# Condition numbers loaded once, W1's masks behind c's low halves, signs for two quarters, and 120 constant products ahead of the first conditioning

## What is computed

```
w = weights[conditions]                               # [128, 64, 64]
c = einsum('bct,bcd->bdt', x, w)                      # x: [128, 64, 512]
def ternarize(W):                                     # W1: [2048, 512], W2: [512, 2048]
    delta = 0.05 * max|W|; mask = |W| > delta
    alpha = sum(|W| where mask) / max(count(mask), 1)
    return alpha * sign(W) * mask
h = gelu(c @ ternarize(W1).T + b1)                    # exact gelu
y = h @ ternarize(W2).T + b2
scale = max|y| / 7 + 1e-8
out = x + clip(round(y / scale), -7, 7) * scale
```

## Time and profile before

| | |
|---|---|
| median of 3 runs | 1003.65 us (1003.36 to 1004.45) |
| the profiled execution | 1004.09 us |
| its span | 1002.2 us |
| PE busy | 925.8 us (92%) |
| DVE busy | 644.5 us (64%) |
| ACT busy | 547.3 us (55%) |
| POOL busy | 144.8 us (14%) |
| mean granted clock | 0.974 |

### The profile page before, as it was taken

How to read it: one execution, slowest core, us unless ns; L and a number is a source line. 1 busy time by engine, 2 the same in 40 slices (tenths; PEclk the granted TensorE clock), 3 DMA queues, 4 the chain that set the end, 5 groups by cost and what they waited for, 6 DMA issues and landing times.

```text
span 1002.2 us, 14662 instructions
## 1 busy us (share of the span) xinstructions
PE 925.8 (92%) x5136; PEld 440.1 (44%) x5136; DVE 644.5 (64%) x1024; ACT 547.3 (55%) x690; POOL 144.8 (14%) x187
## 2 busy tenths in 40 slices
PE   2999999999999999999999999999999999999700
PEld 2544444444444444444444444444444444444300
DVE  7998576665656666656657666665666665633493
ACT  6886728274473827365372827446382836536190
POOL 4400030301203030200203030110303030000000
PEclk9999999999999999999999999999999999999955
DMA  9501103012212102111210301121210301204899
GB/s 341 154 2 43 43 14 82 10 42 44 50 42 51 43 10 59 32 45 42 52 42 25 69 10 42 46 48 42 52 42 10 69 23 44 84 0 168 313 385 390
DMA packets 24318, 77.86 MB, mean 78 GB/s; under 512 B 3952, under 2 KB 4080, under 8 KB 23792
## 3 DMA queue, kind: packets, MB, share of 16 engines
q1 hardware_dynamic: 20032, 73.41, 24.6%
q0 software_dynamic: 3840, 3.94, 1.4%
q10 hardware_dynamic: 432, 0.34, 0.1%
HBM read 60.89 MB, written 16.78 MB: 77 GB/s over the span
## 4 chain that ended last, share of the span: by engine, by line
PE 80%; issue 9%; DVE 5%; ACT 2%; DMA 1%; POOL 0%; SPq 0%; DVEq 0%; POOLq 0%; ACTq 0%
PE ps L433 39%; PE ps L443 37%; PE ps L413 3%; PE ps L494 3%; ACT y L706 1%; DMA y<-in_L_ffn_W 1%; DVE st L907 1%; DVE wts L866 1%; DVE wts L1046 1%; DVE wts L756 1%; DVE y L1046 0%; SPq L275 0%; DVE yc L772 0%; POOL odd L354 0%; DVE wts L911 0%
## 5 line engine op out<-in xcount | busy, mean ns | idle before, releaser
L433 PE MATMUL ps<-yc,wts 128*128 128x512 f16 x2048 | 444.9, 379 | 0.0
L443 PE MATMUL ps<-wts 128*128 128x512 f16 x1792 | 391.4, 379 | 0.0
L433 PEld LDWEIGHTS ps<-yc,wts 128*128 128x128 f16 x2048 | 200.4, 98 | 241.5 <-ACT g L610 0.4
L756 DVE SCALAR_TENSOR_TENSOR wts<-g,st,wts 128x512 f16<-128x512 f32 x256 | 186.4, 749 | 140.2 <-ACT wts L615 138.5
L610 ACT ACTIVATE g<-ps,b1t,st 128x512 f32<-128x512 f32 x256 | 197.9, 774 | 123.3 <-PE ps L433 106.7
L443 PEld LDWEIGHTS ps<-wts 128*128 128x128 f16 x1792 | 173.4, 98 | 204.8
L615 ACT ACTIVATE wts<-g,st 128x512 f16<-128x512 f32 x256 | 181.0, 713 | 0.0
L597 ACT ACTIVATE xs<-yx,st 128x2048 f16<-128x2048 f32 x28 | 56.1, 2002 | 136.8 <-DVE st L790 136.8
L365 POOL PARTITION_ALL_REDUCE st<-st x46 | 21.8, 473 | 663.3 <-DVE st L725 416.1
L348 POOL DMA_INDIRECT odd<-in_L_cond_weights,odd x112 | 110.1, 983 | 41.5 <-issue 30.0
L761 DVE SCALAR_TENSOR_TENSOR y<-ps,st,b2b 128x512 f32 (+1 forms) x56 | 41.6, 747 | 79.8 <-PE ps L443 79.7
(11 more groups left out here) (131 smaller groups left out, 366.8 us busy)
## 6 DMA issues: line engine op xcount, KB each, us to landing
yx<-in_x SPq DMA_DIRECT2D x56, 512.0 KB, 6.3
wts<-in_x SPq DMA_DIRECT2D x10, 512.0 KB, 5.4
out<-wts SPq DMA_DIRECT2D x10, 512.0 KB, 14.0
y<-in_L_ffn_W SPq DMA_DIRECT2D x8, 512.0 KB, 8.8
wts<-in_x SPq DMA_DIRECT2D x4, 1024.0 KB, 5.0
y<-in_L_ffn_W SPq DMA_DIRECT2D x4, 1024.0 KB, 20.5
y<-in_x SPq DMA_DIRECT2D x3, 1024.0 KB, 9.4
out<-wts SPq DMA_DIRECT2D x3, 1024.0 KB, 13.0
```

The costliest lines, as they stand in the source:

```text
L433: last = nc.tensor.matmul(psH[:, j % HB, :], T1T[:, j // HC, k, j % HC * P:(j % HC + 1) * P], csp[:, a, k, :], start=(k == 0 and a == 0), ...
L443: last = nc.tensor.matmul(psY[:, r % 2, :], hsp[:, a, j, r * P:(r + 1) * P], T2T[:, j, :], start=(j == 0 and a == 0), stop=(j == HT - 1 an ...
L756: nc.vector.scalar_tensor_tensor(out=hsp[:, 1, j, :], in0=g[:, j % HB, :], scalar=s_h, in1=hsp[:, 0, j, :], op0=ALU.mult, op1=ALU.subtract ...
```

## The change

- The condition numbers are loaded as one row. DVE clamps the row, PE spreads it to 128 partitions with a product with a row of ones (into hidden tile 0's bank), and DVE makes the row numbers from there.
- x for block 0 is loaded ahead of the last two pieces of W1. b1 is issued behind ACT's first magnitude, b2 as before behind the last. ACT spreads block 0's weights and sums x ahead of the last two magnitudes, and the high halves of c ahead of all relus.
- POOL reduces the bound on c ahead of W1's maximum. DVE makes the scale of c ahead of the threshold. Masks 1 to 3 of W1 stand behind the low halves of c and the rest of quarter 0.
- The count of W1's masks is 64 products with one column each, behind hidden tile 2, and its partition sum is made in the all-reduce of the sums. The second conditioning stands behind hidden tile 3 instead of tile 0; its copies stand beside gelu 8 and 11.
- Quarters 2 and 3 of the ternary W1 are made as sign (ACT) times mask (DVE, f16). The first ternary quarter of W2 is made in two parts, with a signal for the first.
- PE runs 120 products of a constant tile, whose result isn't used, ahead of the first conditioning.

```diff
-        condb, idx, ids = odd_i[:, 0:B], odd_i[:, B:2 * B], odd_i[:, 2 * B:2 * B + BB]
+        cond_row, idx, ids = odd_i[0:1, 0:B], odd_i[:, B:2 * B], odd_i[:, 2 * B:2 * B + BB]
-        psN1, psN2 = psH[:, HB - 1, :], ps[:, HB, 0:1]
+        psN1, psN2 = psH[:, HB - 1, 0:1], ps[:, HB, 0:1]
+        psIds = psH[:, 0, 0:B]
...
-            load_weight(w1s, W1.rearrange("p c k h -> p (c k h)"), LOADS, w1_loaded)
+            load_weight(w1s, w1_v, LOADS, w1_loaded, range(LOADS - 2))
             load_direct(0)
+            load_weight(w1s, w1_v, LOADS, w1_loaded, range(LOADS - 2, LOADS))
             load_direct(1)
...
+            pool.wait_ge(x0_summed, 1)
+            all_max(xwb_part, 1, xwbr, xwb, xwb_all)
             all_max(max1_part, 1, m1r, m1, max1_all)
             gather_direct(1, range(2, RT))
-            pool.wait_ge(x0_summed, 1)
-            all_max(xwb_part, 1, xwbr, xwb, xwb_all)
             pool.wait_ge(sum1_part, 1)
-            nc.gpsimd.partition_all_reduce(rs1r, rs1s, P, RADD).then_inc(sum1_all, 1)
+            nc.gpsimd.partition_all_reduce(sum1r, sum1, P, RADD).then_inc(sum1_all, 1)
...
             def count1(c):
                 pe.wait_ge(mask1_made, c + 1)
-                for n in range(WCH):
-                    last = nc.tensor.matmul(psN1, twos[:, :], quarter(mask1, c, n), start=(c == 0 and n == 0),
-                                            stop=(c == WCH - 1 and n == WCH - 1))
+                for n in range(QUARTER // P):
+                    last = nc.tensor.matmul(psN1, mask1[:, c * QUARTER + n * P:c * QUARTER + (n + 1) * P], twos[:, 0:1],
+                                            start=(c == 0 and n == 0), stop=(c == WCH - 1 and n == QUARTER // P - 1))
...
+            pe.wait_ge(id_row_made, 1)
+            nc.tensor.matmul(psIds, ones_f[0:1, :], id_row, start=True, stop=True).then_inc(ids_spread, 1)
             pe.wait_ge(consts_made, 1)
+            for _ in range(120):
+                nc.tensor.matmul(psH[:, 1, 0:P], twos[:, :], twos[:, :], start=True, stop=True)
             pe.wait_ge(xdirect_loaded[0], 16)
             pe.wait_ge(w_spread, 1)
             condition_direct(0, 0, psC)
             condition_direct(0, 1, psC0)
-            for c in range(WCH):
-                count1(c)
+            pe.wait_ge(idx_made, 1)
             pe.wait_ge(c0_split, 2)
             for j in range(HT):
...
                 if j == HB - 1:
+                    for c in range(WCH):
+                        count1(c)
                     pe.wait_ge(n_read, 1)
                 first(0, j, wait_bank=j >= HB, wait_c=False)
-                if j == 0:
+                if j == HB - 1:
                     pe.wait_ge(xdirect_loaded[1], 16)
...
-            pe.wait_ge(t2_made, 1)
+            pe.wait_ge(t2_begun, 1)
...
+            def sign1(c):
+                part = slice(c * QUARTER, (c + 1) * QUARTER)
+                nc.scalar.activation(t1_flat[:, part], w1s[:, part], ACT.Sign).then_inc(sign1_made, 1)
-            for c in range(LOADS):
+            for c in range(LOADS - 2):
                 absolute(c)
+                if c == 0:
+                    act.dma_start(b1t[:, :], b1).then_inc(b1_loaded, 16)
...
             spread_w(0)
...
+            for c in range(LOADS - 2, LOADS):
+                absolute(c)
+            act.dma_start(b2b[:, :], b2.rearrange("(a n) -> a n", a=1).to_broadcast([P, T])).then_inc(b2_loaded, 16)
+
+            high_c0(0, psC)
+            high_c0(1, psC0)
             act.wait_ge(delta1_ready, 1)
             act.wait_ge(w1abs_made, LOADS)
             relu1(0)
-            high_c0(0, psC)
-            high_c0(1, psC0)
             relu1(1)
             act.wait_ge(c_made, 2)
             spread_w(1)
             relu1(2)
             relu1(3)
+            sign1(2)
...
             def beside_first(j):
-                if j in (3, 5):
+                if j == 3:
+                    sign1(3)
+                if j in (8, 11):
...
+            nc.vector.tensor_scalar(id_row, idt, 0.0, float(S - 1), ALU.max, ALU.min).then_inc(id_row_made, 1)
+            dve.wait_ge(ids_spread, 1)
+            link(nc.vector.tensor_scalar(idx[:, :], psIds, float(C), pc64, ALU.mult, ALU.add))
...
+            def signed1(c):
+                dve.wait_ge(sign1_made, c - 1)
+                dve.wait_ge(mask1_made, c + 1)
+                nc.vector.tensor_tensor(quarter(t1_flat, c), quarter(t1_flat, c), quarter(mask1, c), ALU.mult).then_inc(t1_made, 1)
+            mask_w1(0)
             ternary1(0, slice(0, 1), t1_begun)
             low_c0(0, psC)
             low_c0(1, psC0)
             ternary1(0, slice(1, HC))
+            mask_w1(1)
+            mask_w1(2)
+            mask_w1(3)
+            ternary1(1)
             dve.wait_ge(n1_counted, 1)
-            nc.vector.tensor_reduce(n1, psN1, AX.X, ALU.add).then_inc(n_read, 1)
-            ternary1(1)
-            ternary1(2)
+            nc.vector.tensor_copy(sum1[:, 1:2], psN1).then_inc(n_read, 1)
             dve.wait_ge(relu_summed, WCH)
...
             scale_h(0, link)
+            signed1(2)
-            ternary1(3)
             low_h(0, 0)
             for c in range(WCH):
                 last = max_w2(c)
+                if c == 1:
+                    signed1(3)
...
-            ternary2(0)
+            ternary2(0, slice(0, 2), t2_begun, WCH)
+            ternary2(0, slice(2, HC))
```

More of the change, by code:

```diff
@@ L182, in build @@
         dl1, nd1, dl2, nd2 = stat(), stat(), stat(), stat()
-        rs1, rs1s, rs1r = stat(WCH), stat(), stat()
-        n1, n1c, sm1, alpha1, alpha1p = stat(), stat(), stat(), stat(), stat()
-        rs2, at2 = stat(2 * WCH), stat(WCH + 1)
+        rs1, sum1, sum1r = stat(WCH), stat(2), stat(2)
+        n1c, sm1, alpha1, alpha1p = stat(), stat(), stat(), stat()
+        rs2, at2 = stat(2 * WCH), stat(WCH + 2)
         sum2, sum2r = stat(2), stat(2)
@@ L218, in build @@
         zero_made = sem("zero_made")
+        id_row_made, ids_spread = sem("id_row_made"), sem("ids_spread")
+        sign1_made, t2_begun = sem("sign1_made"), sem("t2_begun")
         diagonal_cleared, w_spread = sem("diagonal_cleared"), sem("w_spread")
@@ L269, in load_half, with load_weight @@
                         .then_inc(xd_loaded, 16)
-            def load_weight(to, source, pieces, loaded):
+            def load_weight(to, source, pieces, loaded, which):
                 size = KT * H // pieces
-                for c in range(pieces):
+                for c in which:
                     part = slice(c * size, (c + 1) * size)
                     sp.dma_start(to[:, part], source[:, part]).then_inc(loaded[c], 16)
-            load_weight(w1s, W1.rearrange("p c k h -> p (c k h)"), LOADS, w1_loaded)
+            w1_v = W1.rearrange("p c k h -> p (c k h)")
+            load_weight(w1s, w1_v, LOADS, w1_loaded, range(LOADS - 2))
             load_direct(0)
+            load_weight(w1s, w1_v, LOADS, w1_loaded, range(LOADS - 2, LOADS))
             load_direct(1)
-            load_weight(w2s, W2.rearrange("p j n -> p (j n)"), WCH, w2_loaded)
+            load_weight(w2s, W2.rearrange("p j n -> p (j n)"), WCH, w2_loaded, range(WCH))
             load_half(0, 2 * DIRECT)
@@ L842, in _ @@
                 last = max_w1(c)
-                if c == 0:
+                if c == 2:
                     dve.wait_ge(b1_loaded, 16)
                     nc.vector.tensor_reduce(xwb[:, 2:3], b1t[:, :], AX.X, ALU.max, apply_absolute_value=True)
+                if c == LOADS - 3:
+                    dve.wait_ge(wd_gathered[0], 16 * RT)
+                    nc.vector.tensor_reduce(xwb[:, 1:2], wg[:, 0:RT, :], AX.XY, ALU.max, apply_absolute_value=True).then_inc(xwb_part, 1)
             link(last)
             nc.vector.tensor_reduce(m1, wm1, AX.X, ALU.max).then_inc(max1_part, 1)
+            dve.wait_ge(xwb_all, 1)
+            link(nc.vector.tensor_scalar(bxw0, xwbr[:, 0:2], TINY0, None, ALU.max))
+            link(nc.vector.tensor_scalar(bits(pxw0), bits(bxw0), EXPONENT, None, ALU.bitwise_and))
+            link(nc.vector.tensor_scalar(pc, pxw0[:, 0:1], float(2 * C), pxw0[:, 1:2], ALU.mult, ALU.mult))
+            link(nc.vector.reciprocal(rc, pc))
+            nc.vector.tensor_scalar(s_c, rc, TOP, None, ALU.mult).then_inc(cscale_ready, 1)
+            nc.vector.tensor_scalar(mr[:, 1:2], pc, 2.0 / P, None, ALU.mult)
             dve.wait_ge(max1_all, 1)
@@ L907, in max_w2, with ternary2, part @@
                 return nc.vector.tensor_reduce(wm2[:, c:c + 1], quarter(w2s, c), AX.X, ALU.max, apply_absolute_value=True)
-            def ternary2(c):
-                link(nc.vector.tensor_scalar(quarter(neg2, c), quarter(w2s, c), nd2, None, ALU.is_lt))
-                nc.vector.scalar_tensor_tensor(out=quarter(t2_flat, c), in0=quarter(w2s, c), scalar=dl2, in1=quarter(neg2, c),
-                                               op0=ALU.is_gt, op1=ALU.subtract, accum_out=at2[:, c:c + 1]).then_inc(t2_made, 1)
-            ternary1(3)
```

(10 more changed lines are left out.)

36 lines of the change are left out of this document (10 added, 26 removed).

## The result

The changed kernel took 1005.48 us (median of 20 runs, 1004.67 to 1007.11) where the kernel before took 1004.04 (20 runs, 1003.36 to 1005.91): a ratio of 1.0015 with a 95% interval of 1.0009 to 1.0021. By the 0.2% named ahead this is no change that counts, on the slower side by 1.4 us. The profiled execution took 1004.78 us around a span of 1003.0, so it was one of the shortest of the twenty. Its mean granted clock is 0.973; the other nineteen have 0.969 to 0.971.

What follows compares the result with a forecast made beforehand. TensorE, busy 92% of the span, was taken as the bound. The first matrix would still end at 60.6, but VectorE's chain would delay the restart 0.7 us, to 64.2: 1004.35 us, same, range 1002.5 to 1006.9 leaving out two in ten.

Steps and rivals of the forecast that it cites:

- Forecast: Whole kernel: restart of the second matrix 0.7 us later, 1004.35 us, same; chance 0.46, own range 1003.2 to 1005.4.
- Start: Before hidden tile 0: earlier indices and conditioning, thresholds 3.2 us later, tile 0 at 26.45 instead of 29.37, 2.9 us gained.
- products of sign and mask: Ternary W1 quarters 2 and 3 on VectorE: 1.28 us each replaces 2.34; at 2.34 another 1.1 us.
- Landings: Loads at the start: b1 holds the maxima until about 13.4, x's first block at about 16.2, last W1 piece at 19.1.
- The stop at the count: Hidden tile 3 waits for VectorE's count read at 34.2, starts 34.4; TensorE idles 0.9 us, first matrix still ends at 60.6.
- The split of the ternary quarter: W2's first ternary quarter in two parts: costs 0.25 us, pair 3.68; the earlier signal at 57.4 buys nothing.
- The 120 products: Ahead of the first conditioning: raise the clock after 6.1 us, end at 15.1, conditioning 17.3 to 21.1; nothing on the path.
- The rival that the prediction gave 0.36: Idle 5.35 us before hidden tile 0 drops the clock, slowing tiles 0 to 2: +2.2 us, 1006.5; chance 0.36.
- list of signs: Signs of being wrong: 16-bit product at 2.3 us, tiles 0 to 2 over 400 ns, W1 maxima past 21, tile 3 before 33.5.
- the length of the low stretch: After a clock fall at tile 0: 6.1 us of work to leave the lower level; were it only 3 us, +0.8.
- 5.1 us of idleness: Read at the kernel's end: this much idleness lets the clock fall, so a hole of about 5 us decides.
- All behind it moves by as much: After the first block: whatever the second matrix's restart shifts, everything later shifts equally.

Runs made afterwards that it cites:

- the second measurement: The unaltered changed kernel run again beside the kernel before, on another occasion, eleven times: median +2.57 us against the kernel before, ratio 1.0023.
- x_sum_first: Changed kernel with ScalarE's sum over x ahead of spreading block 0's weights, and block 1's spreading behind all relus: +1.18 us against the kernel before, ratio 1.0010.
- holes_short: Changed kernel with 170 constant products ahead of the first conditioning instead of 120, and 40 behind it: +0.91 us against the kernel before, ratio 1.0008.
- low_between: Changed kernel with low halves 9 to 11 between the two parts of W2's first ternary quarter: 1005.13 us, +1.18 against the kernel before, ratio 1.0008.
- no_products: Changed kernel without its 120 constant products: +0.93 us against the kernel before, ratio 1.0009.
- three_mended: Changed kernel with the edits of holes_short and low_between, and the second conditioning ahead of the wait for the count's read: 1004.17 us, ratio 1.0000.
- before_low_between: Kernel before with W2's first ternary quarter in two parts and low halves 9 to 11 between them: -0.34 us against the kernel before, ratio 0.9994.
- five_mended: three_mended plus the edits of x_sum_first: +1.91 us against the kernel before, ratio 1.0010.
- six_mended: five_mended with ScalarE's high half of x for the second half block beside block 1's hidden tile 7 instead of 5: +1.79 us, ratio 1.0013.

## Why the prediction was right, and where it was not

*Forecast.* No change that counts, on the slower side, with the time inside the range: that held. The forecast was +0.7 us; measured were +1.44 and, in the second measurement, +2.57. But the case that the forecast is worked out for, in which the clock stays up, is seen in none of the 31 executions of the change (see "The clock"), so that the number came near it is in part luck.

*Start.* The products of sign and mask took 1.22 us against the 1.28 taken; the Trainium skill's figure (VectorE: DVE Perf Modes, The perf-mode tier table) is that number. The gathered weights (16.25 for 16.3) and the conditioning from 17.3 to 21.1 came as written, the indices a little earlier (5.8 for 6.2). Landings were mis-sized to the careful side: b1 was there at 10.3 instead of 13.4, x's first block by 14.2 instead of 16.2 (in x_sum_first, where ACT waits for it), and the last two maxima of W1 ran from 16.59 to 18.9 where they were to end at 20.35. The sum over x then set the scale, and tile 0 started at 25.87 instead of 26.45.

*The stop at the count.* The step holds: tile 3 waits for the read, at 34.73 for 34.4 forecast. But the number was met by two errors that cancel. With the clock up the read stands at 33.24 and 33.37, a microsecond earlier than the sum said; in the first profile the clock put 1.17 back. So the +0.7 of the forecast was not the chain's: in the two profiles with the clock up until the read (holes_short and the second of the change), the second count is 0.25 to 0.30 later than before. The other 0.8 us of the first profile's 1.09 came with the clock.

*The split of the ternary quarter.* Its two parts take 4.08 us (56.38 to 60.46) against 3.7, a little more than the 0.25 set down. I wrote that the earlier signal buys nothing, which is true as the change is ordered; low_between shows that the split is worth more than a microsecond at the restart once the low halves stand between its parts.

*The 120 products.* "This gives nothing on the path" held. That they end at 15.1 did not: they ended at 17.0 in the first profile, with gaps of up to 1.1 us waiting for issue, and at 14.4 in the second, without. The pace rose sooner than after the 6.1 us taken from the kernel before: from 22 products in 2 us to 27 between 8 and 10 us in the first profile, and to 36 between 10 and 12 us in the second.

*The clock.* The rival that the prediction gave 0.36 is what the first profile shows, at its place, with 1.17 us instead of 2.2. Its list of signs named tiles 0 to 2 at over 400 ns a product: eight of the 24 start 427 ns apart. Two of its terms failed. It took the length of the low stretch from the first conditioning (6.1 us); after every fall ahead of 40 us the clock was back after some 3.4 us. And it took 5.1 us of idleness from the end of one trace as what decides. Over the fourteen profiles, the fall at the end of the kernel comes 2.4 to 5.2 us after the last product, the 5.2 being that very trace, and in holes_short it is 2.4, as its timeline of PE and its windows from 947 us show:

```profile
917.90 27.79 PE L553 MATMUL ps<-wts 128*128 128x512 f16 x128
...
947.00:948.00 1.00, 0.00 (x0) 1.00 0.99 348
948.00:949.00 1.00, 0.00 (x0) 0.57 1.09 426
```

At the start it fell in the hole of 2.6 us of no_products and didn't in the 3.36 us of the second profile of the change. So these holes don't divide by their length alone.

The further mistake was to treat the fall as one case beside the forecast and to look at one hole. In the twelve profiles of the change and the kernels made from it, falls lie among the constant products or around the start of the conditioning (eight profiles, 14.8 to 17.1 us), at tile 0 (six, 25.0 to 26.8), and within some 1.5 us behind the count, in the work that follows it (three, 34 to 36); only holes_short and three_mended have none at the start. The Trainium skill (TensorE: Matmul & The Clock Gate, Part 1: The HAM clock gate) says that the point at which the array's activity is looked at runs free of the kernel; the two profiles of one program agree, with a fall near 26.5 us in one and falls near 17 and 34 us in the other. The Trainium skill names idleness there as what lets the clock fall; no_products shows that a short hole is enough.

What the executions without a profile did can be read from their mean granted clock: 0.001 of it is some 2 us at the lower level (an estimate: 0.001 of 1003 us, over the 0.5 between the levels). The executions of the kernel before in the three later measurements have 0.972 to 0.975, nearly all of the loss being the stretch behind its last product. The profiles without a fall at the start have 0.973 or 0.974. The first profile of the change has 0.973 with one fall; the other thirty executions of the change have 0.968 to 0.971. So each of them had at least one. Eighteen of the thirty have 0.970 or less, and all five profiles at 0.970 show two; the first profile is a mild case.

*"All behind it moves by as much."* This holds only roughly. Three_mended gains 1.6 us at the second count and 0.5 at the last product, but x_sum_first, 0.15 later than the kernel before at the second count, is 1.08 later at the last product, while before_low_between keeps 0.89 of its 1.17. From the one mark to the other the thirteen profiles lose between nothing and 1.1 us against the kernel before's; one execution of each can't say how much of that belongs to the order.

What stays open: the group of the changed kernel's times at +2.2 us and more. A fall at tile 0 explains about 1.1 us at the second count. No profile of a kernel with 120 products and the change's ternary quarters shows more than that: in low_between the products meet the pauses and the low clock and end at 18.5, but tile 0 started at 25.8 there all the same. five_mended, with 170 products, shows a heavier case, late products and late conditioning together, 1.7 us at the second count. That the group goes with more low stretches the mean clocks do show: in the second measurement of the change the three short executions have 0.970, seven of the eight long ones 0.968 or 0.969. In five_mended three executions at 0.974 took 1002.52 to 1003.07 and the nine at 0.970 or 0.971 took 1004.11 to 1006.63; in six_mended the only one at 0.974 took 1002.39, those at 0.972 and 0.973 took 1003.90 to 1004.22, the rest 1005.19 and more. What isn't told apart is the low clock itself and the pauses in the constant products, which in five_mended's profile come together. Holes_short supports the clock less than its 0.91 against 2.57 suggests: in the first measurement the change itself lay at +1.44, it was not run on the chip of holes_short, and six of the eleven executions of holes_short have 0.971 or less, so the clock fell in many of them too.

## What to carry to other kernels

Ahead of the first dense stretch ask where TensorE will be idle after the edit, not only what becomes earlier: a hole of a few microseconds can cost as much as it won, and it does so in some executions only, so one profile doesn't settle it. The mean granted clock of the executions without a profile says whether the profiled one is typical. A fixed number of filler products guards one hole and delays what follows as soon as the clock or the supply of instructions is slower than planned. And before a start is made earlier, look for the engine whose chain ends at the next restart: here 1.1 us less for VectorE behind the count's read was worth 1.0 at the restart, and 3.5 us at tile 0 were worth nothing.

## What was not expected of the hardware

- 64 products with one column each behind 24 full ones, then 0.7 us of waiting, and the granted clock went to 0.50 some 0.7 us into the next tile (0.55 over 34 to 36 us in the second profile of the change). The same sequence, with waits of 0.3 to 0.7 us, kept the clock up in the other profiles that have it.
- The idle time ahead of a fall is no fixed number: 2.3 us in the hole of no_products, 5.2 us at the end of the kernel before, 2.4 us at the end of holes_short.
- A straight run of 120 or 170 products met pauses of 0.3 to 1.1 us marked as issue between 10.7 and 15 us in eight of the eleven profiles of kernels that have it, while the DMA share was about 1.0. The three without pauses are the three taken on one chip; all eight from elsewhere have them. In the second profile of the change the run took 9.40 us without pauses, in the first 12.1 with them.
